# Centering folded into the turn of the tokens: a kernel with a convolutional recurrence and a mixture of experts

## The reference

```
x = x + conv_recurrence(layernorm over channels(x))
t = tokens(x)                      # 16 x 1024 tokens of 64 channels
t = t + experts(layernorm over channels(t))
x = from_tokens(t)
```

```
pooled = einsum('bked,bke->bed', gathered, topv)     # gathered: normed tokens
h   = gelu(einsum('ebd,edh->ebh', [pooled, 1], weight1))
out = einsum('ebh,eho->ebo', [h, 1], weight2)        # scattered back, weighted
```

## Time and profile before

| | us |
|---|---|
| median of 3 runs | 206.62 |
| lowest, highest | 203.53, 207.08 |
| the profiled execution | 206.3 |
| its span, first to last instruction | 204.5 |

### The profile page before, as it was taken

One profiled execution on the slowest core, in us unless ns is written; L12 is line 12 of the kernel. 1 busy time (PEld: TensorE's weight loads), 2 busy tenths in 40 slices (PEclk: granted clock), 3 DMA queues, 4 the chain that ended last, 5 costly groups with the idle time before them and its releaser, 6 DMA issues.

```text
span 204.5 us, 10877 instructions
## 1 busy us (share of the span) xinstructions
PE 178.7 (87%) x4687; PEld 147.9 (72%) x4687; DVE 164.3 (80%) x605; ACT 109.9 (54%) x266; POOL 125.5 (61%) x113
## 2 busy tenths in 40 slices
PE   1789996999999989999999999999997988998900
PEld 1578875799869978987999798888874776684200
DVE  0768797999999898899889968888889999445960
ACT  2373435665666555667556566666457696640000
POOL 4443549598987989698898899579248930000000
PEclk9999999999999999999999999999999999999975
DMA  4955090422423143251441342432180131000896
GB/s 104 186 111 109 10 199 11 107 58 58 102 59 84 33 104 103 62 103 33 133 108 34 83 106 58 118 98 56 53 194 19 51 107 51 6 3 8 232 350 235
DMA packets 29120, 19.12 MB, mean 94 GB/s; under 512 B 2464, under 2 KB 28048, under 8 KB 29072
## 3 DMA queue, kind: packets, MB, share of 16 engines
q1 hardware_dynamic: 27440, 15.87, 31.1%
q10 hardware_dynamic: 1632, 2.56, 4.1%
HBM read 14.12 MB, written 4.30 MB: 90 GB/s over the span
## 4 chain that ended last, share of the span: by engine, by line
PE 63%; DVE 18%; issue 5%; POOL 4%; DMA 2%; ACT 2%; SPq 1%; DVEq 0%; POOLq 0%
PE ps L946 42%; PE ps L937 10%; PE ps L1006 4%; POOL r L404 3%; DMA w_rows<-in_L_conv_w_stos 2%; PE ps L1073 2%; DVE ps L715 2%; DVE tail_room L930 2%; DVE xtok L930 2%; DVE lg L871 2%; DVE x_split L866 2%; DVE st L674 2%; DVE cands L860 1%; PE ps L1194 1%; PE ps L1238 1%
## 5 line engine op out<-in xcount | busy, mean ns | idle before, releaser
L946 PE MATMUL ps<-x_split,w_hi 64*64 64x256 f16 x1000 | 50.3, 273 | 2.0 <-DVE fc L718 1.1
L382 POOL TENSOR_TENSOR xc<-xc,h 128x256 f32<-128x256 f32 x31 | 22.6, 728 | 22.8 <-DVE h_lo L699 22.8
L946 PEld LDWEIGHTS ps<-x_split,w_hi 64*64 64x64 f16 x1000 | 25.9, 107 | 13.5 <-issue 8.7
L715 DVE TENSOR_TENSOR ps<-sg_i,ps 64x256 f32<-64x256 f32 x62 | 26.6, 430 | 8.8 <-ACT ps L515 7.3
L946 PE MATMUL ps<-h_hi,w_lo 64*64 64x256 f16 x750 | 32.4, 272 | 0.8 <-issue 0.8
L946 PE MATMUL ps<-h_lo,w_hi 64*64 64x256 f16 x750 | 32.2, 272 | 0.0
L946 PE MATMUL ps<-h_hi,w_hi 64*64 64x256 f16 x750 | 32.1, 272 | 0.0
L499 ACT ACTIVATE ps<-ps,bias 128x256 f32<-128x256 f32 x32 | 14.3, 448 | 32.8 <-PE ps L946 32.8
L404 POOL TENSOR_TENSOR r<-v,pow_exp 128x16 f32<-128x16 f32 x7 | 20.6, 2936 | 8.5 <-DVE v L668 8.5
L946 PE MATMUL ps<-x_split,w_lo 64*64 64x256 f16 x500 | 24.9, 270 | 0.0
L937 PE MATMUL ps<-ident,xc 128*128 128x128 f32 x128 | 18.5, 289 | 6.9 <-DMA xc<-in_x 5.4
(11 more groups left out here) (130 smaller groups left out, 329.8 us busy)
## 6 DMA issues: line engine op xcount, KB each, us to landing
xc<-in_x SPq DMA_DIRECT2D x14, 256.0 KB, 4.0
rb_xr<-scratch SPq DMA_DIRECT2D x14, 256.0 KB, 4.4
w1s<-in_L_ffn_weight SPq DMA_DIRECT2D x8, 256.0 KB, 3.6
w2s<-in_L_ffn_weight SPq DMA_DIRECT2D x8, 256.0 KB, 3.2
rbf<-scratch SPq DMA_DIRECT2D x24, 64.0 KB, 2.4
out<-xtok SPq DMA_DIRECT2D x4, 256.0 KB, 5.4
out<-xtok ACTq DMA_DIRECT2D x4, 256.0 KB, 5.9
out<-tail_room SPq DMA_DIRECT2D x3, 256.0 KB, 4.4
```

Of the source, the lines that this page charges most:

```text
L382: p.tensor_tensor(here, here, h32[:, i % 2, :].rearrange("p (b w) -> p b w", w=W), ALU.add) \
L715: v.tensor_tensor(ps_ig[half(h), :], sg_i[half(1 - h), :], pre[G][half(1 - h), 0:COLS], ALU.mult) \
L946: ins = pe.matmul(pre[gate][to, 0:COLS], w[half(h), tap, C * GATE_ORDER[gate]:][:, 0:C], data[half(h)], start=first and m == 0, stop=s_don ...
```

## The change

A new matrix `centering` is built once by GpSimd: -1/64 in each of the two 64x64 blocks on the diagonal, 0 elsewhere, plus the identity. In `turn_x1` each transpose against the identity becomes a product with `centering`: the tokens come out turned and with their mean subtracted. DVE's two operations that centered the pooled tokens go, and the semaphore between them changes its name. Everything else stays.

```diff
+            p.memset(centering[:, :], 0.0).then_inc(s_centering, 1)
+            p.wait_ge(s_centering, 1)
+            for h in range(2):
+                p.memset(centering[half(h), half(h)], -1.0 / C).then_inc(s_centering, 1)
+            p.wait_ge(s_centering, 3)
+            p.wait_ge(s_const, 2)
+            p.tensor_tensor(centering[:, :], centering[:, :], ident[:, :], ALU.add).then_inc(s_centering, 1)
...
             for g in range(NG):
                 v.wait_ge(s_pooled, g + 1)
                 v.tensor_scalar(pooled[:, g, :], POOL_BANKS[g][:, 0:C], rsum[:, g:g + 1], None, ALU.mult) \
-                    .then_inc(s_centered, 1)
-                v.wait_ge(s_centered, 3 * g + 1)
-                v.tensor_reduce(pmean[:, g:g + 1], pooled[:, g, :], AX.X, ALU.add).then_inc(s_centered, 1)
-                v.wait_ge(s_centered, 3 * g + 2)
-                v.scalar_tensor_tensor(pooled[:, g, :], pmean[:, g:g + 1].to_broadcast([128, C]), -1.0 / C,
-                                       pooled[:, g, :], ALU.mult, ALU.add).then_inc(s_centered, 1)
+                    .then_inc(s_pool_scaled, 1)
...
                 wait(pe, s_xtok, 2 * u)
+                pe.wait_ge(s_centering, 4)
                 for k in range(2):
                     pe.wait_ge(s_x_stats, min(2 * (u + AHEAD) + k + 1, 2 * NT))
                     for b in range(4):
-                        ins = turn(ps_t[k][:, 128 * b:128 * b + 128], xc[:, 4 * k + b, u, :], 128)
+                        ins = pe.matmul(ps_t[k][:, 128 * b:128 * b + 128], xc[:, 4 * k + b, u, :], centering[:, :],
+                                        start=True, stop=True)
                     ins.then_inc(s_x1_turned, 1)
...
-                pe.wait_ge(s_centered, 3 * g + 3)
+                pe.wait_ge(s_pool_scaled, g + 1)
                 ins = turn(PT_BANK[0:C, 128 * g:128 * g + 128], pooled[:, g, :], 128)
```

More of the change, by code:

```diff
@@ L75, in metaformer @@
         ident = sb("ident", [128, 128])
+        centering = sb("centering", [128, 128])
         w_rows = sb("w_rows", [128, 2, 2, 3 * C])
@@ L175, in metaformer @@
         s_pool_room = sem("s_pool_room")
+        s_centering = sem("s_centering")
         s_conv_w_in = sem("s_conv_w_in")
@@ L254, in metaformer @@
         s_pooled = sem("s_pooled")
-        s_centered = sem("s_centered")
+        s_pool_scaled = sem("s_pool_scaled")
         s_pooled_turned = sem("s_pooled_turned")
```

## The result

| | before | after |
|---|---|---|
| median, us | 205.26 (6 runs, 203.53 to 207.08) | 210.8 (6 runs, 210.41 to 213.35) |
| the profiled execution | 206.3, span 204.5 | 210.53, span 208.7 |

The change makes the kernel slower: ratio 1.033, 95% interval 1.0275 to 1.0391. The ratios here leave out executions that took over 1.5% more than the fastest of the same kernel, the medians do not, so the medians of the table, divided, give 1.027. The forecast was 213.2 us, range 210.0 to 217.0, slower with a chance of 0.88. "Before" now has three more runs than when the prediction was made, and their median is 1.4 us lower than the 206.62 of then.

What follows compares the result with a forecast made beforehand. TensorE's own work was taken to bound the kernel. Loop 6.1 + last turn 0.8 + pooled tokens 0 + start 0 = 6.9 us, added to the profiled 206.3, gave 213.2 us, range 210.0 to 217.0.

Steps and rivals of the forecast that it cites:

- The bound: Whole loop: TensorE, at full clock, works almost without waits; other engines release it for only 0.5 us.
- Price of a turn: Eight token products per turn, two instructions each, make a turn 0.87 + 0.05 = 0.92 us longer.
- factor of four: Skill's claim that fp32 transposes are four times faster than products; a turn would grow 2.6 us, not 0.92.
- The loop: Seven token turns in the loop: six at 0.92 us, tile 2 at 0.54, sum 6.1 us.
- tile 2: Loop turn where TensorE's wait for DVE's `fc`, 0.38 us, is eaten first, leaving 0.54 of 0.92 us.
- The last turn: Token turn at 154.95 us, on the chain: delays the scaled logits by 0.8 us, between 0.49 and 0.92.
- The pooled tokens: Last pooled group: removing DVE's centering gains 0, since first_bias occupies TensorE; ends 0 and 0.33 us.
- The start: GpSimd's building of the matrix, 1.7 us at most, fits its 4.37 us idle before 7.60; cost 0.
- Loads show: Token turns: weight loads stick out 0.048 us per instruction, 219 us (8%); wholly serial loads, 226 us (5%).
- Mostly hidden: Loop: ScalarE and DVE's round trip sets the period; half hidden 210 us, wholly 207; chance 8%.
- Not slower: Token turns: a product passes as one instruction of 0.109 us like a transpose; 206.0 us; chance 3%.
- The signs: Profile after: 128 matmuls about 0.109 us apart, 1.9 us per turn, no tile 2 wait, scaled logits at 166.1.

Runs made afterwards that it cites:

- experiment 3: The kernel before, with each of the 64 token transposes issued twice into the same place; 210.92 us, ratio 1.0281.
- experiment 12: The change, with each token product split into two of 64 tokens side by side in the array; 211.35 us, ratio 1.0266.
- 10: The change, with 9 real products of a zeroed tile on TensorE ahead of the image; 210.8 us, ratio 1.0281 to the kernel before.
- 8: The kernel before, with 9 real products of a zeroed tile on TensorE ahead of the image; 207.19 us, ratio 1.0033.
- experiment 1: The change, with DVE's sum and subtraction of the pooled means kept; 211.84 us, ratio 1.031 to the kernel before.
- experiment 2: The kernel before, without DVE's sum and subtraction of the pooled means, turns still transposes; 205.45 us, ratio 0.9962.
- 4: The change, with plain transposes for the last tile's token turn alone; 211.96 us, ratio 1.0301 to the kernel before.
- 11: The change, with first_bias(0) moved behind the last pooled turn; 212.17 us, ratio 1.0317 to the kernel before.
- 5: The kernel before, with first_bias(0) moved behind the last pooled turn; 205.99 us, one run.
- 6: The kernel before, with first_bias(0) behind the last pooled turn and without DVE's sum and subtraction of the pooled means; 206.38 us, one run.
- 7: The kernel before, with 12 transposes of the identity on TensorE ahead of the image; 205.03 us, ratio 1.0004.
- 9: The kernel before, with 6 real products of the identity on TensorE ahead of the image; 205.56 us, ratio 1.0031.

## Why the prediction was right, point by point

- **The bound.** Right: TensorE's own work set the period, and waits for other engines in the loop stayed at 0.5 us. That the clock is full "from the first slice" was wrong. The start runs at half the clock for a time that differs from execution to execution, and the page does not show it. The sum did not rest on it, but the spread did. The profiled execution of before had a start 1.7 us longer (1.0 of it clock), 0.7 more in issue gaps and 0.3 more at the end, so the spans differ by 4.2 where the parts that belong to the change make 6.9.
- **Price of a turn.** Forecast 0.92, measured 0.96: 16 instructions 0.112 apart instead of 0.109, and a first load of 0.102 instead of 0.105. Experiment 3 shows 0.87 of it as plain streaming, experiment 12 the last 0.09 as the wide load. The Trainium skill's factor of four ("TensorE: Matmul & The Clock Gate", section Terms) did not hold: a product takes 2 x 0.112 = 0.223 us against 0.109 of the transpose, a factor of two.
- **The loop.** Forecast 6.1; measured 6.2 without the issue gaps, 5.7 between experiments 10 and 8, 5.6 for plain doubling (experiment 3, 120.4 - 114.8). Two terms were a little off, in opposite directions. A turn costs 0.96, not 0.92. And what the longer turn eats was forecast as 0.38, all at tile 2; measured against the periods of experiment 1 it is 0.30 in the tile that begins with turn 2 and 0.24 in that of turn 6, which was not counted: 7 x 0.96 - 0.54 = 6.2. The reason given for tile 2 fits all traces. There the operation of 1.08 us starts 0.03 us ahead of the turn before and costs 0.30; in experiment 2 it starts 0.40 behind it and the tile is 0.72 longer; in the five kernels with whole products (after, 1, 4, 10, 11) it starts 0.36 to 0.38 ahead, and the tile is no longer than its neighbours, but for the gap after. So what is eaten differs from execution to execution, and one trace could not give it. As they ran, the loops of these five last 121.1 us in the mean and the seven with single transposes (before, 2, 5 to 9) 115.9: 5.2 apart. Six of the seven have issue gaps there, one of the five has; whether the change makes them rarer or that is chance is not shown.
- **The last turn.** Forecast 0.8, measured 0.92 to the scaled logits (5.14 against 4.22; 4.22 again in experiment 4). "Between 0.49 and 0.92" was decided by TensorE alone, its upper end, because the filler in front of the spread has no room. Behind it 0.2 comes back, which was not foreseen: DVE's long operation no longer meets GpSimd's. That is the last turn's doing too: from the scaled logits to the pooled turns it takes 16.71 us before and in experiment 4, 16.50 to 16.60 in the change and in experiments 1, 3, 10 and 11.
- **The pooled tokens.** Forecast 0, and 0 in experiments 1 and 2. The reason held too: experiments 5 and 6 take the cover away and the 0.5 us appears.
- **The start.** Forecast 0 for GpSimd's four operations: they end at 4.31, and the first power starts at 7.50, before 7.60.
- **The rivals.** "Loads show" wanted 0.048 us more per instruction; it is 0.003. "Mostly hidden" is refuted by the periods: without the gaps five grow by 0.95 to 0.97, and the other two by 0.66 and 0.72. "Not slower" wanted one instruction per product; there are two.
- **The signs.** The 128 matmuls of their own line are there, 0.112 apart (0.115 was the limit), with 1.98 us to the next state product (1.9 was said), the wait at tile 2 is gone, and the last pooled turn stands 0.65 behind `first_bias`. The scaled logits were to start at 166.1 and start at 163.89, since the start and the gaps were taken as equal in both executions. One sign of being wrong, a turn that adds less to the period than to TensorE, came true in the tile of turn 6, by 0.24.
- **The total.** By the two profiled executions, gaps taken out, the change costs 6.2 + 0.92 - 0.2 = 6.9 us, and 6.9 were forecast. That it agrees to the tenth is partly luck: with the mean loops as they ran it is 5.2 + 0.92 - 0.2 = 5.9. The totals lie on both sides: the medians are 5.5 apart, and the ratio says 0.033 x 205.26 = 6.8 us. The forecast stood on the profiled execution of 206.3, about 1 us above the median of six runs, so 213.2 came out above the 210.8 measured.

## What to carry to other kernels

Folding arithmetic into a transpose is not free: in fp32 a real product issues two instructions where the transpose issues one, and where TensorE sets the period that is paid in full each time, but for what a wait there already took, here 0.96 us per eight turns. A wait that the trace names is won only if nothing else stands in its place: look at what else its engine has in flight (here the bias product) before counting it. And where the start of a kernel differs from one execution to the next, compare stretches of the trace between the same two points, not spans. What a gap in a pipelined stream costs is read off the period of its tile, not off the idle time that the trace prints: here 1.12 us for a gap of 0.84.

## What the runs showed of the hardware that was not expected

- **The clock at the start.** TensorE runs at half its clock at first and goes up at times that differ: the same 16 matmuls at 10 us take 1.85 us in one execution and 1.04 in another. The page's clock line shows full speed there; the distance between matmuls of one shape tells. How it goes up is not settled.
- **Gaps put down to issue come with the loading of TensorE's instructions.** TensorE's stream has now and then one gap of 0.15 to 1.3 us put down to issue, in another place in nearly each kernel, or none. Before, in the weight loads, and after, in the timeline, and the page's line on the DMA queue that brings instructions:

```profile
76.42 0.11 PEld L946 LDWEIGHTS ps<-h_hi,w_lo 64*64 64x64 f16 x2 [1.11 <-issue]
...
57.34 0.11 PEld L951 LDWEIGHTS ps<-h_hi,w_hi 64*64 64x64 f16 x1
...
57.88 0.25 PEld L951 LDWEIGHTS ps<-h_hi,w_hi 64*64 64x64 f16 x11 [0.42 <-issue]
...
q8 instruction: 37, 0.61, 1.2%
```

  In the page's line, q8 is the queue, 37 its packets and 0.61 their megabytes. The 37 packets have 16,384 bytes each, and TensorE has 9,486 records before, sequencer's included: 256 to a packet. The 14 traces have 21 such gaps in TensorE's row, beside the 0.58 ahead of the first state product and the 1.51 ahead of the last turn, which stand at the same place in the program. Counted by TensorE's records, all 21 end at the 193rd or 194th place of a row of 256, and in each a packet of q8 had landed 1.2 to 1.6 us before (at 75.13 for 76.42, at 56.35 for 57.88). This agreement says that TensorE stood still because the next 256 instructions came late; no experiment moved them. What makes them late in one execution and not in another is not shown.
- **DVE beside GpSimd.** An operation on 16 columns takes 1.08 us, and ends just behind GpSimd's operation (kernel after, timeline):

```profile
53.41 2.04 POOL L425 TENSOR_TENSOR xtok<-xtok,r 128x512 f32<-128x512 f32 x2
...
54.42 1.08 DVE L672 SCALAR_TENSOR_TENSOR v<-st 128x16 f32<-128x16 f32 x1
```

  GpSimd's two end at 55.45, DVE's at 55.50. Other calls of the same line tell more: of its 193 operations on 16 columns in the 14 traces, the 56 that start while GpSimd scales the tokens take over 1.0 us, and the other 137 under 0.2. The 1.42 us of line 871 is the same pattern: 1.42 or 1.43 in the eight traces where GpSimd's operation has 0.34 us left at its start, 1.21 in the six where it has ended or has 0.09 left. That one holds up the other is read from this agreement; no experiment moved one of them.
